# The conditioning vector q computed in two parts: 16 sequences before the second x tile, 112 after it

## The reference, cut to what matters

```python
# x: (128 sequences, 32 positions, 256), cond: (128, 128)
q_emb = relu(cond @ W3 + b3)                      # one vector of 256 for each sequence
v_sum = sum(x, axis=1, keepdims=True)             # over the 32 positions
c = relu(((32 * x + v_sum) * q_emb[:, None, :]) @ W2 + b2)
w1q, w3q, w2q = ternary(w1), ternary(w3), ternary(w2)   # each from the mean of its absolute values
out = x + (silu(c @ w1q.T) * (c @ w3q.T)) @ w2q.T       # hidden width 682
```

## Time and profile before

| | before |
|---|---|
| median of 3 runs | 165.79 us (165.62 to 165.82) |
| the profiled execution's own time | 165.22 us |
| its span in the profile | 163.4 us |
| TensorE matmul busy | 159.5 us, 98% |
| VectorE busy | 118.7 us, 73% |
| ScalarE busy | 89.1 us, 55% |
| GpSimd busy | 55.1 us, 34% |

### The profile page before, as it was taken

The page is one execution under the profiler, slowest core; times in us unless marked ns, Lnnn a source line. Parts: engine busy times, 40 slices in busy tenths (PEclk is TensorE's granted clock), DMA queues, the critical chain, the costliest instruction groups (busy, mean ns, idle before and its releaser), DMA issues.

```text
span 163.4 us, 2290 instructions
## 1 busy us (share of the span) xinstructions
PE 159.5 (98%) x760; PEld 131.0 (80%) x760; DVE 118.7 (73%) x190; ACT 89.1 (55%) x163; POOL 55.1 (34%) x53
## 2 busy tenths in 40 slices
PE   8999999999999999999999999999999999999992
PEld 4798777888887888788887888788887888788892
DVE  1698999988978892798458891788548870566863
ACT  4077889344845375445844475345844466255540
POOL 5014022502460276205750276204841266001500
DMA  5998656665666599200240007000150006000163
GB/s 138 330 337 161 95 83 98 97 98 85 97 98 98 89 201 169 34 4 0 49 79 0 4 0 128 2 0 0 35 96 4 2 0 117 12 0 0 21 112 128
DMA packets 67412, 12.67 MB, mean 78 GB/s; under 512 B 63216, under 2 KB 67144, under 8 KB 67400
## 3 DMA queue, kind: packets, MB, share of 16 engines
q1 hardware_dynamic: 67248, 12.46, 39.2%
q10 hardware_dynamic: 152, 0.07, 0.2%
HBM read 8.32 MB, written 4.19 MB: 77 GB/s over the span
## 4 chain that ended last, share of the span: by engine, by line
PE 97%; DVE 1%; issue 0%; DVEq 0%
PE bank L553 50%; PE bank L596 22%; PE bank L483 15%; PE bank L580 3%; PE bank L469 2%; PE bank L518 1%; PE bank L445 1%; PE bank L498 1%; PE bank L452 1%; PE bank L510 0%; DVE qT L769 0%; PE bank L492 0%; PE bank L443 0%; DVE x L682 0%; DVE xo L821 0%; PE bank L521 0%
## 5 line engine op out<-in xcount | busy, mean ns | idle before, releaser
L553 PE MATMUL bank<-c_hi,T 128*128 128x512 f32 (+1 forms) x176 | 69.2, 393 | 0.0
L553 PE MATMUL bank<-c_lo,T 128*128 128x512 f32 (+1 forms) x176 | 68.8, 391 | 0.0
L389 ACT ACTIVATE silu<-bank,checked 128x512 f32<-128x512 f32 (+1 forms) x48 | 33.1, 689 | 51.5 <-PE bank L553 51.4
L806 DVE SCALAR_TENSOR_TENSOR gf<-bank,out_scale,silu 128x512 f32<-128x512 f32 (+1 forms) x42 | 31.2, 744 | 34.4 <-PE bank L553 30.8
L553 PEld LDWEIGHTS bank<-c_hi,T 128*128 128x128 f32 (+1 forms) x176 | 32.8, 186 | 7.6 <-issue 0.2
L553 PEld LDWEIGHTS bank<-c_lo,T 128*128 128x128 f32 (+1 forms) x176 | 32.8, 186 | 7.3
L272 POOL TENSOR_TENSOR x<-y,qT 128x512 f32<-128x512 f32 x12 | 13.7, 1144 | 53.2 <-DVE y L711 53.2
L596 PE MATMUL bank<-g_hi,T 128*128 128x512 f32 x70 | 28.5, 407 | 0.0
L814 DVE TENSOR_TENSOR g_lo<-gf,g_hi 128x512 fp32r<-128x512 f32 x40 | 28.5, 711 | 0.0
L396 ACT CAST g_hi<-gf 128x512 fp32r<-128x512 f32 x40 | 24.5, 612 | 5.4 <-DVE gf L806 5.1
L596 PE MATMUL bank<-g_lo,T 128*128 128x512 f32 x70 | 27.3, 390 | 0.0
(11 more groups left out here) (81 smaller groups left out, 118.1 us busy)
## 6 DMA issues: line engine op xcount, KB each, us to landing
xb<-in_x_dram SPq DMA_DIRECT2D x64, 64.0 KB, 2.5
out_dram<-turned SPq DMA_DIRECT2D x28, 128.0 KB, 2.7
xo<-in_x_dram SPq DMA_DIRECT2D x3, 256.0 KB, 4.4
w_sb<-in_L_ffn_w_dram SPq DMA_DIRECT2D x2, 384.0 KB, 5.5
w_sb<-in_L_ffn_w_dram SPq DMA_DIRECT2D x1, 682.0 KB, 7.8
w_sb<-in_L_ffn_w_dram SPq DMA_DIRECT2D x2, 256.0 KB
xo<-in_x_dram SPq DMA_DIRECT2D x1, 512.0 KB, 4.7
xo<-in_x_dram SPq DMA_DIRECT2D x2, 128.0 KB, 2.4
```

Of the source, the lines that this page charges most:

```text
L389: nc.scalar.activation(silu[r, m % 2, :], h1[j % 2][r], ACT.Silu, scale=checked[r, 0:1]).then_inc(silu_done, 1)
L553: last = pe.matmul(dst[j % 2][0:w, :], T13[:, k, col:col + w], part[:, g % NC, k, :], start=(i == 0), stop=(i == len(passes) - 1))
L806: nc.vector.scalar_tensor_tensor(out=gf[r, m % 3, :], in0=second, scalar=out_scale[r], in1=silu[r, m % 2, :], op0=ALU.mult, op1=ALU.mult). ...
```

## The change

q is computed in two parts. QF = 16 sequences (halves 0 and 1) are projected where all 128 were, into bank 5, and VectorE adds the bias and clips for these 16 alone. The other 112 are projected after `mix_x(0)`, in the place of the three filler matmuls, into bank 4, and ScalarE adds the bias and clips, in the gap before its `relu(0)`. A new semaphore `q_rest_ready` tells that this is done; VectorE waits for it in `scale_mixed` (halves 2 and 3), TensorE before `sum_partitions(0)`, which writes bank 4.

```diff
+    QF = HALVES * HB
-        qT_ps = bank[:, 5, 0:DC * B].rearrange("p (c b) -> p c b", c=DC)
+        q_first_ps = bank[:, 5, 0:DC * QF].rearrange("p (c b) -> p c b", c=DC)
+        q_rest_ps = bank[:, 4, 0:DC * (B - QF)].rearrange("p (c b) -> p c b", c=DC)
# ScalarE
             act.wait_ge(b_cols_copied, 1)
+            act.wait_ge(q_done, 2 * DC)
+            for c in range(DC):
+                nc.scalar.activation(qT[:, HALVES:NH, c, :], q_rest_ps[:, c].rearrange("p (h b) -> p h b", b=HB), ACT.Relu,
+                                     bias=b3_col[c]).then_inc(q_rest_ready, 1)
# TensorE
                     if n == 0 and t == 1:
                         transpose_b()
-                        project_q()
+                        project_q(q_first_ps, slice(0, QF))
-            def project_q():
+            def project_q(q_ps, sequences):
                 pe.wait_ge(got_W3, 16)
                 pe.wait_ge(condT_copied, 1)
                 for c in range(DC):
-                    pe.matmul(qT_ps[:, c, :], W3_sb[:, c * P:(c + 1) * P], condT[:], start=True, stop=True
+                    pe.matmul(q_ps[:, c], W3_sb[:, c * P:(c + 1) * P], condT[:, sequences], start=True, stop=True
                               ).then_inc(q_done, 1)
             mix_x(0)
-            keep_busy(3)
+            project_q(q_rest_ps, slice(QF, B))
             mix_x(1)
...
             pe.wait_ge(const_ready, 4)
+
+            pe.wait_ge(q_rest_ready, DC)
             sum_partitions(0)
# VectorE
             def scale_mixed(n):
+
+                dve.wait_ge(q_rest_ready, DC)
...
             for c in range(DC):
-                nc.vector.tensor_scalar(qT[:, :, c, :], qT_ps[:, c, :].rearrange("p (h b) -> p h b", b=HB), b3_col[c], 0.0,
-                                        ALU.add, ALU.max).then_inc(q_ready, 1)
+                nc.vector.tensor_scalar(qT[:, 0:HALVES, c, :], q_first_ps[:, c].rearrange("p (h b) -> p h b", b=HB), b3_col[c],
+                                        0.0, ALU.add, ALU.max).then_inc(q_ready, 1)
```

More of the change, by code:

```diff
@@ L163, in adaln_ternary_ffn_kernel @@
         b_cols_done, b_cols_copied = sem("b_cols_done"), sem("b_cols_copied")
-        q_done, q_ready = sem("q_done"), sem("q_ready")
+        q_done, q_ready, q_rest_ready = sem("q_done"), sem("q_ready"), sem("q_rest_ready")
         abs_done, sums_done, limit_done = sem("abs_done"), sem("sums_done"), sem("limit_done")
```

## The result

| | before | after |
|---|---|---|
| median | 165.68 us (164.86 to 166.14, 22 runs) | 166.19 us (165.12 to 167.57, 22 runs) |
| ratio | 1 | 1.0043, 95% interval 1.0024 to 1.0062 |
| profiled execution, its span | 165.22 us, 163.4 us | 167.34 us, 165.5 us |

The changed kernel is slower by 0.5 us in the median. The spread says more than the median: the 22 times of before lie within 1.3 us of each other, those of after within 2.5 us. Ten of the 22 are at 166.91 us or above, where before has none, and three are at 165.12 or 165.13. Six lie between 165.90 and 166.30; no profile was taken of one of these.

A forecast was written before the change was run, and what follows sets the result against it. TensorE, busy 98% of 163.4 us, was taken as the bound; a 0.20 us earlier start, mostly lost to a new wait, left about 0.1: 165.22 - 0.09 = 165.13 us profiled, median 165.79 to 165.70, range 165.45 to 165.96.

The forecast's parts named there:

- the cost of the narrow q matmuls on TensorE's pace: First q matmuls on TensorE: 16 columns take as long in the queue as 128, with no cost to the pace counted.
- rival (4): TensorE's pace rises later, behind `mix_x(1)`: 1.3 us lost less 0.1 won, 167.0 us; chance 0.07.
- q matmuls paced by weight loads: First q matmuls on TensorE: still 0.11 us apart with 16 columns, so the second x tile is not earlier.
- rival (3): Weight loads don't pace narrow matmuls: second x tile 0.34 us earlier, w3 load limits the gain to 0.22, 165.57; chance 0.03.
- The shorter tail: From the last q matmul's start to VectorE's start: 0.28 us in place of 0.38, so VectorE's q starts 0.10 earlier.
- VectorE's q: Bias and clip on VectorE: some 0.235 us for 16 columns where 128 take 346 ns, 0.11 us less, twice.
- What is late next: VectorE's x1 of half 0 then waits for the mixing, 0.38 us behind its last start: gain 0.20, not 0.32.
- The rest of q on TensorE: Four matmuls of 112 columns in the fillers' place: 0.45 us for 0.17, so `mix_x(1)` is put back by 0.28.
- the wait: VectorE's sum of half 1 waits for the later `mix_x(1)`: 0.16 of the 0.20 us, about 0.1 stays on TensorE.
- rival (1): Half 1's mixing is in time or VectorE catches up: TensorE's whole 0.20 us stays, 165.59 us; chance 0.14.
- ScalarE: nothing: The rest of q's bias and clip on ScalarE: two operations of 0.2 to 0.42 us before `relu(0)`, costing nothing.
- Downstream: Absolute values of w3 on ScalarE, bound by the w3 load: at most 0.22 us passes there, so 0.1 passes.

The follow-up runs named there:

- e4: The changed kernel run again, unaltered: 165.37 us, ratio 1.001, 5 of 12 runs above 166.4 us.
- e1: The changed kernel with the first q matmuls 128 columns wide again, VectorE still reading 16: 165.44 us, ratio 0.9987.
- e5: e3 with 16 columns in the four q matmuls and the other sequences' q left out: 166.50 us, ratio 1.0018.
- e3: The kernel before with only q's bias and clip split, 16 columns on VectorE, 112 on ScalarE: 165.39 us, ratio 0.9986.
- h4: e3 repeated, the same kernel: 165.53 us, ratio 1.0000, 1 of 12 runs above 166.4 us.
- e6: The changed kernel with two fillers ahead of the transpose of the biases: 165.37 us, ratio 0.9988, 4 of 12 runs above 166.4 us.
- e7: The kernel before without the two fillers behind the transpose of cond: 165.78 us, ratio 1.0001.
- f3: e3 without its three fillers behind `mix_x(0)`: 165.39 us, ratio 1.0003.
- h2: The kernel before with two added matmuls of 128 columns, output unused, ahead of q: 166.02 us, ratio 1.0027.
- g1: e3 with the load of W2 issued ahead of that of half 1: 165.63 us, ratio 1.0014.
- e8: e3 with 64 columns in the four q matmuls and the other sequences' q left out: 166.80 us, ratio 1.0041.
- h1: The kernel before with two added matmuls of 16 columns, output unused, ahead of q: 167.30 us, ratio 1.0070.
- f2: e3 with 112 columns in the four q matmuls and the other sequences' q left out: 165.43 us, ratio 1.0006.

## Why the prediction was wrong

The median of 166.19 us lies above the range of 165.45 to 165.96, and the side was wrong too: I gave slower a chance of 0.10.

- **The failed step is the cost of the narrow q matmuls on TensorE's pace.** The sum took them as free, since four of 16 columns take as long in the queue as four of 128, and let the pace rise where it did before. The case in which it doesn't was rival (4), seen but given too little weight. Its place was right, the narrow q at the edge of the slow stretch, and its sign. I gave it 0.07, with the argument that "only four short instructions differ" and "nothing idle is added". What the runs showed in its place: the four narrow matmuls are the cause, with 5 late runs of 12 against none (e4 and e1) and 7 against none (e5 and e3), and in effect something idle is added: the pace of four weight loads stays, the streaming beside them goes. I had worked out that very fact, that narrow matmuls still start 0.11 us apart, as a reason why nothing is won, and didn't read it as a reason why TensorE streams less.
- **One trace was taken for all.** I had the rise between 4.14 and 5.45 us from one execution and asked whether it would move. In the profiles of this study it moves by itself, for one kernel too (e3 and h4, after and e4). I place it, to about 0.1 us, where the float32 weight loads of 128 columns go from 0.33 to 0.19 us. In the eleven profiles with an early rise it lies at 3.9 (e6), 4.2 to 4.4 (e1), 4.3 to 4.5 (e4, e7), 4.5 (h4), 4.7 (e5), 4.9 (f3), 5.2 (before, e3), 5.6 (h2) and 6.2 us (g1). In the seven late ones it lies between 9.8 (e8) and 10.3 (h1), and in none between 6.2 and 9.8. In the three profiles with the narrow q and an early rise it came before or just as q began (q starts at 4.48 in e6, 4.67 in e4, 4.71 in e5). In the five of f3, before, e3, h2 and g1 it came 0.1 to 1.5 us behind the first of these wide matmuls. That fits a picture in which the executions whose rise would fall behind the start of a narrow q lose it; with so few profiles it is a reading and no proof. The Trainium skill, "TensorE: Matmul & The Clock Gate", Part 1, says that the point differs from run to run of one kernel; the traces agree (5.2 us in e3, 4.5 in h4).
- **Its price was too low.** I priced it at 1.3 us less 0.1, with a rise behind `mix_x(1)`. The late rise falls in the first projection, at 10.0 in the profile of after: 167.34 against 164.86 us for the two profiled executions of the changed kernel, 2.5 us. The second is the fastest of its kernel; the other early runs of e4, at 165.38 or below, leave about 2.
- **q matmuls paced by weight loads: right.** In the early execution of e4 the q matmuls of 16 columns start at 4.80, 4.91 and 5.03. The gap of 25 ns that the Trainium skill, "TensorE: Matmul & The Clock Gate", section "Back-to-back issue gap", gives for so few columns doesn't appear in q; rival (3) fell. The rows that the prediction took this from were one pair of three. Another pair of L492 in the same trace starts at 11.80 and 11.83, 0.03 apart, behind weight loads that start (0.30 - 0.19) = 0.11 apart. So it is the loads that keep the distance, and two narrow matmuls can stand close together where their loads ran ahead:

```profile
11.69 0.30 PEld L492 LDWEIGHTS bank<-abs_sums,ones 128*128 128x128 f32 x2
11.80 0.28 PE L492 MATMUL bank<-abs_sums,ones 128*128 128x2 f32 x2
11.83 0.25 PE L492 MATMUL bank<-abs_sums,ones 128*128 128x2 f32 x1
```

- **The shorter tail: wrong.** I took 0.28 us from the last q matmul to VectorE. It is 5.41 - 5.03 = 0.38, as with 128 columns. It cost nothing, since q wasn't what x1 waited for any more.
- **VectorE's q: right.** 0.235 us were worked out for each, 228 ns (median) measured in the profile of after:

```profile
L780 DVE TENSOR_SCALAR qT<-bank,b_cols x2: 224/228/233, 5.8 to 5.9; 128x16 f32<-128x16 f32 x2
```

- **What is late next: right.** x1 waits for the mixing, 0.38 us behind its last start (5.55 to 5.93 in e4). Measured from there, the first L476 comes at 6.53, 0.98 later; before it was 6.94 - 5.79 = 1.15. That is a gain of 0.17 where the sum had 0.20.
- **The rest of q on TensorE: right in size.** It takes 0.44 us of the queue (5.66 to 6.10 in e4) for 0.45 in the sum, and makes VectorE wait 0.13 for 0.16. **Too much was made of the wait:** from the first to the second L476 it is 8.74 - 6.53 = 2.21 us, before 2.24. So the loss of 0.1 there didn't come: from the last start of the mixing the second L476 comes 8.74 - 5.55 = 3.19 us later, before it was 9.18 - 5.79 = 3.39. That is the 0.20 of rival (1), where the sum kept 0.1.
- **ScalarE: nothing, right.** Two operations of 0.35 us in an idle stretch, done at 6.96 in e4, 1.5 us ahead of `relu(0)`:

```profile
6.36 0.60 ACT L328 ACTIVATE qT<-bank,b_cols 128x112 f32<-128x112 f32 x2 [2.65 <-PE bank L459]
8.51 0.84 ACT L338 ACTIVATE ct<-bank,b_cols 128x256 f32<-128x256 f32 x2 [1.55 <-PE bank L476]
```

- **Downstream: the right kind of limit, too short a list.** I named the load of w3. The loads of W2 (e3), of half 3 (e1) and, once W2 went first, of half 1 (g1) bind in one execution or another. That may be why the 0.2 us of e1 and e3 don't show up as a clear gain; no run took these waits away together.

So without the late rise the forecast of no change would have stood: e1, which differs from the change only in the width of the first q matmuls, is at 0.9987 (0.9970 to 1.0005).

## What to carry to other kernels

While TensorE is still at half pace, narrowing a matmul behind a full weight load saves no time in its queue and can cost the rise: here 16 columns for 128 in four instructions cost 2 us in nearly half of the runs and 0.5 in the median. At half pace, from the first start of q to the last start of the second tile, it is 1.66 us with 16 columns (4.63 to 6.29, after) and 1.66 with 112 (4.84 to 6.50, f2). Take the shorter dependent operation (here VectorE's 16 columns) and leave the matmul wide; that made 1 late run of 24 (e3 and h4), though no clear gain either. Where the ramp of a kernel matters, look at the spread of many runs and the starts of equal instructions in several profiles, since one profile shows only one of the possible rises.

## What the runs showed of the hardware

The start-to-start distance of equal matmuls doubled and halved (0.43 and 0.22 us for L476) under a granted clock of 1.00, so the granted clock in the profile isn't enough to find the slow stretch. In the 18 profiles of this case the rise came either by 6.2 us or not before 9.8. A hole of about 0.87 us (four weight loads with 16 columns each, 4.80 to 5.67 in h1) made 8 of 12 runs late, while the loss of the two fillers near 3.2 us (e7) or of the three behind q (f3) made none. Why the place counts so much, and what bf16 fillers are worth there, stays open.
